# The last layer's causal mask: zeros selected by GpSimd in the exponentials, in place of mask products by TensorE in the exponent step

## The chip, the core and the metric

The kernel runs on one core of a Trainium2 chip. The metric is the device time in microseconds (us) of one execution; lower is better. Five engines of the core run in-order instruction streams side by side and meet at semaphores: TensorE (PE, matrix products into the eight PSUM banks), VectorE (DVE), ScalarE (ACT, activation functions), GpSimd (POOL, elementwise work on SBUF tiles, it does not read PSUM here) and SyncE (SP, which issues the transfers).

## The reference, cut to what matters

Four blocks are added to x in turn: a softmax attention of x over a context, an attention whose projections are a mixture of experts, a rotary cross attention, and a last layer. The last layer is the one that the change touches. It has 16 heads of 8 channels, 16 sequences of 128 tokens, a causal mask, and behind it a mixture of eight experts:

```
wei = jnp.einsum('bhtf,bhsf->bhts', q, k) * d ** (-0.5)
mask = jnp.tril(jnp.ones((t, t), bool))
wei = jnp.where(mask, wei, -jnp.inf)
wei = jax.nn.softmax(wei, axis=-1)
attn = jnp.einsum('bhts,bhsf->bhtf', wei, v)
...
y = x + layernorm(attn, ln1_g, ln1_b)
combine = top-2 of softmax gates;  h = relu(y W1 + b1);  moe = sum_e combine_e (h W2 + b2)_e
out = y + layernorm(moe, ln2_g, ln2_b)
```

## The kernel before

**Tiling.** The 16 sequences are worked in eight jobs of SPS=2 sequences. Five lanes (0 to 4) hold a job each, with buffers of their own; lanes 0 to 2 take a second job afterwards. A sixth lane (5, MOE) runs the expert products of one job after the other, and a seventh splits W1 at the start. `way(lane)` lists a lane's steps, and the string `ORDER` says, one digit per step, which lane goes next. All engines walk the same list `STEPS`, each issuing its own part of a step, so a step's place in the list is its place in every engine's stream. `TAKEN` deals out the PSUM banks in the same way.

**Attention of a layer L (B, C or D).** For each of the two sequences there is a step M: TensorE makes the scores with the query in the partitions, in four banks (q = 0 to 3, four heads each), and VectorE takes the maximum of each row (L1041). The maxima are transposed (hop "mt"). Then come two steps for each sequence. Step E (`scores` with q_first False): TensorE makes the scores again with the key in the partitions, adding the negative maximum by a product with `two` and `mT` (L622, then L630), and ScalarE writes the exponentials of bank after bank to `probs` (L816), a ring of 8 slots of 128x512 that lies in the tile `w1f`. Step PV (`weighted`, L644): TensorE multiplies `probs` by the values, 8 products for each q; it waits for `s_exp` before each q. After the second PV ScalarE copies the result (L823) and hop "pt" transposes it (L548).

**The mask.** In layer D, both M and E put a mask product first: for each of four blocks of 32 partitions and each bank q, one product of a 32x32 table (`lowS`, or `lowST` in E) by a 32x512 spread table adds -60000 to the scores that are to be masked (L613). That makes 16 products for a step; the products after it accumulate on it. There are 16 steps M and 16 steps E in layer D, one for each sequence.

**GpSimd's stream.** GpSimd turns variances into scale and shift of each norm (step ln1, L1075 to L1078; the step moe_end does the same for the last norm), ranks the gate logits (hops "B.lg" and "D.lg", L1086 to L1093), adds rows (L1113, L1129, L1132, L1134), writes `ylo` (L1136) and the output rows (L1144, L1146). It had nothing to do in a step E. ScalarE's normalisation (L781, step ln2) waits for L1078; VectorE's choice of experts (`pick`, L879 to L902) waits for L1093, and TensorE's transpose L567 waits for that.

## Time and profile before

| | |
|---|---|
| median of three runs | 498.88 us (498.03 to 503.34) |
| the profiled execution | 499.3 us, of which the profile's span 497.5 us |
| TensorE (PE) busy | 461.8 us, 93% of the span |
| ScalarE (ACT) busy | 367.8 us, 74% |
| VectorE (DVE) busy | 307.3 us, 62% |
| GpSimd (POOL) busy | 159.9 us, 32% |

The profile is one execution. A "busy" engine has an instruction in flight; the products of TensorE overlap each other, so the sum of their durations is larger than its busy time. A timeline row gives the start in us from the start of the span, the length in us, the engine, the line of the kernel, the operation, the tile written and the tiles read, their shapes, how many instructions of one kind the row merges (x16), and in square brackets how long the engine had been idle before and what released it.

### The profile page before, as it was taken

Reading aid. Unit: us, or ns where it says so; the run is one execution under the profiler, and the core shown is the slowest. Engines: PE = TensorE matmul, PEld = TensorE weight load, DVE = VectorE, ACT = ScalarE, POOL = GpSimd, SP = SyncE. Lnnn points to the kernel's source line nnn. Section 1 sums busy time; section 2 is a strip of 40 time slices with the busy share of each in tenths; the row PEclk is TensorE's granted clock in tenths of the full one; section 3 lists DMA queues with packets and bytes.
Section 4 is the critical chain, followed back from the end, with each engine's and each line's share of the span. In section 5 each row is a group of like instructions: output and inputs, shape, how many; then the busy total and the mean of one; then the engine's idle time right before and its main releaser. Section 6 shows DMA issues by size and latency. Waiting matters only on the chain.

```text
span 497.5 us, 18057 instructions
## 1 busy us (share of the span) xinstructions
PE 461.8 (93%) x7501; PEld 379.9 (76%) x7501; DVE 307.3 (62%) x941; ACT 367.8 (74%) x906; POOL 159.9 (32%) x400
## 2 busy tenths in 40 slices
PE   7768889989989999999999999999999999999793
PEld 5635476666667988897878888898798888899793
DVE  4378997978877774667875684647634736333211
ACT  5586778888888897877779878776977576675452
POOL 6662342123234422326242134141221421332302
PEclk9688999999999999999999999999999999999998
DMA  6930000000000000000000000000000000000000
GB/s 192 389 110 1 9 3 10 9 3 3 3 3 13 2 14 3 13 1 14 2 13 3 3 2 4 13 1 3 14 3 1 3 12 4 1 12 1 12 2 11
DMA packets 7928, 11.38 MB, mean 23 GB/s; under 512 B 592, under 2 KB 7208, under 8 KB 7464
## 3 DMA queue, kind: packets, MB, share of 16 engines
q1 hardware_dynamic: 7848, 10.23, 6.2%
q8 instruction: 60, 0.98, 0.9%
q14 instruction: 20, 0.16, 0.1%
HBM read 9.18 MB, written 1.05 MB: 21 GB/s over the span
## 4 chain that ended last, share of the span: by engine, by line
PE 74%; DVE 13%; POOL 6%; ACT 3%; issue 3%; DMA 0%; POOLq 0%; DVEq 0%; ACTq 0%
PE bk L654 23%; PE bk L644 6%; PE bk L699 6%; DVE negmax L1041 6%; PE bk L700 5%; PE bk L701 5%; PE bk L630 4%; PE bk L585 2%; PE bk L622 2%; PE bk L613 2%; PE bk L548 2%; PE bk L488 2%; PE bk L554 1%; PE bk L534 1%; PE bk L497 1%
## 5 line engine op out<-in xcount | busy, mean ns | idle before, releaser
L654 PE MATMUL bk<-w2f,hT 128*128 128x128 f32 x1024 | 135.6, 276 | 1.0 <-ACT hT L842 1.0
L842 ACT ACTIVATE hT<-bk,pk 128x256 f32<-128x256 f32 x256 | 107.6, 477 | 38.9 <-PE bk L701 38.4
L654 PEld LDWEIGHTS bk<-w2f,hT 128*128 128x128 f32 x1024 | 124.1, 192 | 3.9 <-ACT hT L842 1.3
L1041 DVE TENSOR_REDUCE negmax<-bk 128x4 f32<-128x512 f32 (+1 forms) x192 | 104.9, 610 | 12.7 <-PE bk L630 12.2
L816 ACT ACTIVATE w1f<-bk 128x512 f32<-128x512 f32 (+1 forms) x192 | 98.8, 600 | 18.2 <-PE bk L630 17.9
L972 DVE SCALAR_TENSOR_TENSOR acc<-bk,comb,acc 128x128 f32<-128x128 f32 x128 | 38.8, 344 | 74.9 <-PE bk L654 74.7
L699 PE MATMUL bk<-yhi,w1hi 128*128 128x256 f16 x256 | 70.1, 274 | 0.0
L701 PE MATMUL bk<-yhi,w1lo 128*128 128x256 f16 x256 | 69.8, 273 | 0.0
L700 PE MATMUL bk<-ylo,w1hi 128*128 128x256 f16 x256 | 69.8, 272 | 0.0
L1075 POOL TENSOR_SCALAR shift<-mv 128x2 f32<-128x2 f32 x40 | 9.4, 235 | 143.3 <-DVE mv L982 142.4
L644 PE MATMUL bk<-w1f,val 128*32 128x128 f32 (+1 forms) x1536 | 51.0, 275 | 0.2 <-DVE negmax L1041 0.2
L630 PE MATMUL bk<-qk 32*128 32x128 f16 (+2 forms) x1536 | 46.8, 213 | 1.6 <-DVE hl L1028 0.4
L644 PEld LDWEIGHTS bk<-w1f,val 128*32 128x32 f32 (+1 forms) x1536 | 39.4, 109 | 6.7 <-issue 2.3
L802 ACT ACTIVATE qk<-bk 128x512 f16<-128x512 f32 x72 | 37.9, 603 | 6.0 <-PE bk L585 6.0
L630 PEld LDWEIGHTS bk<-qk 32*128 32x128 f16 (+1 forms) x1536 | 32.1, 96 | 12.5 <-issue 6.5
L1086 POOL TENSOR_TENSOR qkf<-lg 128x16 f32<-128x16 f32 (+1 forms) x32 | 8.4, 284 | 76.9 <-DVE lg L867 44.8
L699 PEld LDWEIGHTS bk<-yhi,w1hi 128*128 128x128 f16 x256 | 25.6, 100 | 6.0 <-issue 1.4
L622 PE MATMUL bk<-hl,hf 32*128 32x128 f16 (+1 forms) x768 | 29.0, 218 | 0.9 <-ACT hl L766 0.5
L1077 POOL TENSOR_TENSOR rstd<-ve,neghalf 128x2 f32<-128x2 f32 x40 | 28.5, 713 | 3.3
L622 PEld LDWEIGHTS bk<-hl,hf 32*128 32x128 f16 (+1 forms) x768 | 19.9, 99 | 10.3 <-issue 7.5
L701 PEld LDWEIGHTS bk<-yhi,w1lo 128*128 128x128 f16 x256 | 25.0, 98 | 2.9
L700 PEld LDWEIGHTS bk<-ylo,w1hi 128*128 128x128 f16 x256 | 25.1, 98 | 2.8
(150 smaller groups left out, 783.7 us busy)
## 6 DMA issues: line engine op xcount, KB each, us to landing
w1f<-in_w SPq DMA_DIRECT2D x1, 2048.0 KB, 15.1
w2f<-in_w SPq DMA_DIRECT2D x1, 2048.0 KB
pk<-in_pack SPq DMA_DIRECT2D x1, 1690.0 KB, 8.1
xin<-in_x SPq DMA_DIRECT2D x8, 128.0 KB, 2.6
out<-outb SPq DMA_DIRECT2D x8, 128.0 KB, 1.8
ctxT<-in_turned SPq DMA_DIRECT2D x8, 77.0 KB, 2.4
cin<-in_ctx SPq DMA_DIRECT2D x8, 77.0 KB
hf<-in_half SPq DMA_DIRECT2D x1, 416.0 KB, 10.4
```

The costliest lines, as they stand in the source:

```text
L622: mm(score_bank(q, t == 0 and L != "D")[0:nk, t * T:(t + 1) * T], H("two")[rows_, t * T:t * T + nk], mT[s][rows_, i * T:(i + 1) * T], star ...
L630: last = mm(o, qs if q_first else ks, ks if q_first else qs, start=q_first and L != "D", stop=L != "D" or t == NT - 1)
L644: last = mm(o[32 * t:32 * t + 32, (2 * i + a) * T:(2 * i + a + 1) * T], val[s][0:nk, m, SHIFT * r:SHIFT * r + 32], probs[0:nk, ring(n, q), ...
L654: last = mm(o[:, i * D:(i + 1) * D], hT[:, k % HRING, i * T:(i + 1) * T], w2f[:, k, :], start=c == 0 and i == 0, stop=c == CH - 1, skip_gr ...
L699: mm(o[:, m * W:(m + 1) * W], hi, yhi[s][:], start=True, stop=False)
L700: mm(o[:, m * W:(m + 1) * W], hi, ylo[s][:], start=False, stop=False)
L701: last = mm(o[:, m * W:(m + 1) * W], lo, yhi[s][:], start=False, stop=True)
L802: act.activation(qk[s][:, :, t, :], bank(g, st, t)[:].rearrange("p (n w) -> p n w", n=2), ACT.Copy).then_inc(s_stk_act, 1)
L816: act.activation(probs[0:nk, ring(n, q), :], bank(g, st, q)[0:nk, :], ACT.Exp, scale=SCALE[L]).then_inc(s_exp, 1)
L842: act.activation(hT[:, k % HRING, :], bank(g, st)[:, m * W:(m + 1) * W], ACT.Relu, bias=P("b1")[:, k:k + 1]).then_inc(s_relu, 1)
L972: last = dve.scalar_tensor_tensor(out=acc[:, i, :], in0=products(j, e)[:, i * D:(i + 1) * D], scalar=comb[j % LANES][:, i, e:e + 1], in1=a ...
L1041: dve.tensor_reduce(negmax[s][:, i, NT * q:NT * (q + 1)], bank(g, st, q)[:, 0:NT * nk].rearrange("p (t k) -> p t k", t=NT), X_AXIS, ALU.ma ...
```

## The change

The exponent step of layer D no longer issues the 16 mask products: `masked` is true for M alone, and in E the product by `two` (L622, now L626) opens the accumulation in each bank instead of L613. The exponentials of layer D therefore hold values also where the mask is to act. GpSimd gets a part in step E of layer D: for q = 0 to 3 it waits for ScalarE's exponential (`s_exp`), runs one `affine_select` over the slot of `probs` in place (128x512, float32: a key later than the query becomes 0.0), and counts up the new semaphore `s_causal`. TensorE's PV in layer D waits for `s_causal` in place of `s_exp`; in layers B and C nothing changes. `TURN` counts the E steps of one layer, as `NUMBER` counts all of them. The five semaphores `s_mixT` of the lanes become one, with `TURN` as its count, which makes room for the new one; the instructions that signal and wait there stay where they were. The tables `lowST` and `spreadST` are still loaded. The string `ORDER` is the same.

```
-        pe.wait_ge(s_mixT[s], g + 1)
+        pe.wait_ge(s_mixT, TURN[g, ("top", s, "B")] + 1)
...
-                if L == "D":
-
-                    low, spread = ("lowS", "spreadS") if q_first else ("lowST", "spreadST")
+                masked = L == "D" and q_first
+                if masked:
+
+                    low, spread = "lowS", "spreadS"
                     for c in range(NT):
...
-                            mm(score_bank(q, t == 0 and L != "D")[0:nk, t * T:(t + 1) * T], H("two")[rows_, t * T:t * T + nk],
-                               mT[s][rows_, i * T:(i + 1) * T], start=L != "D", stop=False)
+                            mm(score_bank(q, t == 0)[0:nk, t * T:(t + 1) * T], H("two")[rows_, t * T:t * T + nk],
+                               mT[s][rows_, i * T:(i + 1) * T], start=True, stop=False)
...
                 for q in range(NQ):
-                    pe.wait_ge(s_exp, NQ * n + q + 1)
+                    if L == "D":
+                        pe.wait_ge(s_causal, NQ * TURN[g, ("E",) + st[1:]] + q + 1)
+                    else:
+                        pe.wait_ge(s_exp, NQ * n + q + 1)
...
+                elif kind == "E" and st[2] == "D":
+                    n = NUMBER[g, st]
+                    for q in range(NQ):
+                        pool.wait_ge(s_exp, NQ * n + q + 1)
+                        p3 = probs[:, ring(n, q), :].rearrange("p (t k) -> p t k", t=NT)
+                        pool.affine_select(p3, p3, [[0, NT], [1, T]], ALU.is_ge, 0.0, base=0, channel_multiplier=-1
+                                           ).then_inc(s_causal, 1)
```

How the streams change. First TensorE's stream at the second E step of lane 0 in layer D; L613 are the mask products, L622 those with the maxima, L630 the scores, and each row is one instruction or several alike, with the semaphores that it waits for. Before:

```order
L613 MATMUL bk<-hf 32x512 [waits s_stk_act]
L613 MATMUL bk<-hf 32x512 [waits s_read4]
L613 MATMUL bk<-hf 32x512 [waits s_stk_act]
L613 MATMUL bk<-hf 32x512 [waits s_stk_dve]
L613 MATMUL bk<-hf 32x512 x12
L622 MATMUL bk<-hl,hf 128x128 x4
L630 MATMUL bk<-qk 128x128 x4
L622 MATMUL bk<-hl,hf 128x128 x4
L630 MATMUL bk<-qk 128x128 x4
L622 MATMUL bk<-hl,hf 128x128 x4
```

After the change (L622 is now L626, L630 is L634):

```order
L626 MATMUL bk<-hl,hf 128x128 [waits s_stk_act]
L626 MATMUL bk<-hl,hf 128x128 [waits s_read4]
L626 MATMUL bk<-hl,hf 128x128 [waits s_stk_act]
L626 MATMUL bk<-hl,hf 128x128 [waits s_stk_dve]
L634 MATMUL bk<-qk 128x128 x4
L626 MATMUL bk<-hl,hf 128x128 x4
L634 MATMUL bk<-qk 128x128 x4
L626 MATMUL bk<-hl,hf 128x128 x4
```

The 16 mask products are gone, and the waits for the four free banks have moved to the first products with the maxima. Next TensorE's stream at the PV step of lane 0 (the weighted values of its first sequence, L644). Before, it waits for the exponentials alone:

```order
L585 MATMUL bk<-hl,hf 128x256 x12
L644 MATMUL bk<-w1f,val 32x128 [waits s_exp]
L644 MATMUL bk<-w1f,val 32x128 x3
L644 MATMUL bk<-w1f,val 32x128 [waits s_exp]
L644 MATMUL bk<-w1f,val 32x128 x3
```

After the change that line is L651; of the same kind of step in layer D:

```order
L588 MATMUL bk<-hl,hf 128x256 x12
L651 MATMUL bk<-w1f,val 32x128 [waits s_causal,s_exp]
L651 MATMUL bk<-w1f,val 32x128 x3
L651 MATMUL bk<-w1f,val 32x128 [waits s_causal]
L651 MATMUL bk<-w1f,val 32x128 x3
```

The two quarters left out go on in the same way. All four groups of products wait for GpSimd now; `s_exp` in the first row is the wait for a free bank. Last GpSimd's stream around the first two E steps of lane 0 in layer D; L1075 to L1078 are the scale and shift of a norm, and L1129 adds a row of constants. Before:

```order
L1076 TENSOR_SCALAR ve<-mv 128x2
L1077 TENSOR_TENSOR rstd<-ve,neghalf 128x2 [waits c_pool]
L1078 TENSOR_TENSOR shift<-shift,rstd 128x2 [waits c_pool]
L1129 TENSOR_TENSOR wc<-wc,rw 128x256 [waits s_xn1]
L1075 TENSOR_SCALAR shift<-mv 128x2 [waits s_mv4]
L1076 TENSOR_SCALAR ve<-mv 128x2
L1077 TENSOR_TENSOR rstd<-ve,neghalf 128x2 [waits c_pool]
L1078 TENSOR_TENSOR shift<-shift,rstd 128x2 [waits c_pool]
L1075 TENSOR_SCALAR shift<-mv 128x2 [waits s_mv3]
```

After the change (L1075 is now L1082, L1129 is L1143):

```order
L1084 TENSOR_TENSOR rstd<-ve,neghalf 128x2 [waits c_pool]
L1085 TENSOR_TENSOR shift<-shift,rstd 128x2 [waits c_pool]
L1139 AFFINE_SELECT w1f<-w1f 128x512 [waits s_exp] x4
L1143 TENSOR_TENSOR wc<-wc,rw 128x256 [waits s_xn1]
L1139 AFFINE_SELECT w1f<-w1f 128x512 [waits s_exp] x4
L1082 TENSOR_SCALAR shift<-mv 128x2 [waits s_mv4]
L1083 TENSOR_SCALAR ve<-mv 128x2
L1084 TENSOR_TENSOR rstd<-ve,neghalf 128x2 [waits c_pool]
L1085 TENSOR_TENSOR shift<-shift,rstd 128x2 [waits c_pool]
```

The selections stand at the place of the E step, four for each, and the norms of lanes 4 and 3 (`s_mv4`, `s_mv3`) stand behind the second four.

## Rows read from the trace of the kernel before

**Rows 1.** The profile's slices: TensorE's busy tenths in 40 slices of the span.

```profile
PE   7768889989989999999999999999999999999793
```

**Rows 2.** Windows: busy us of each engine, then granted clock, DMA share, GB/s.

```profile
125.00:440.00 315.00, 309.24 (x5296) 261.90 (x5295) 196.81 (x601) 245.38 (x598) 98.90 (x241) 1.00 0.02 6
440.00:497.00 57.00, 46.95 (x420) 44.19 (x418) 13.74 (x53) 27.74 (x68) 11.85 (x26) 0.97 0.02 6
```

**Rows 3.** TensorE's waits from 125 to 440 us, longest: total, times, longest.

```profile
PE bk L567 <- DVE comb L902: 1.4, 2, 0.7
```

**Rows 4.** Timeline: the first E step of layer D and its PV.

```profile
125.71 0.43 PE L613 MATMUL bk<-hf 32*32 32x512 f16 x16
126.08 0.23 PE L622 MATMUL bk<-hl,hf 32*128 32x128 f16 x4
126.75 2.06 ACT L816 ACTIVATE w1f<-bk 128x512 f32<-128x512 f32 x4 [0.34 <-PE bk L630]
129.39 0.32 PE L644 MATMUL bk<-w1f,val 128*32 128x128 f32 x4
```

**Rows 5.** GpSimd's groups by shape: count, busy us, mean ns, idle before.

```profile
L1129 POOL TENSOR_TENSOR wc<-wc,rw 128x256 f32<-128x256 f32 x8 | 5.8, 728 | 1.0 <-ACT wc L781 1.0
L1108 POOL MEMSET val<- 128x1024 f32 x5 | 4.8, 952 | 0.0
L1076 POOL TENSOR_SCALAR ve<-mv 128x2 f32<-128x2 f32 x40 | 8.9, 222 | 2.5
L1089 POOL TENSOR_SCALAR qkf<-qkf 128x128 f32<-128x128 f32 x8 | 4.3, 538 | 0.7
L1124 POOL CAST hl<-qkf 128x154 f16<-128x154 f32 x8 | 3.0, 380 | 0.5
```

**Rows 6.** Timeline: the second pair, the norm on GpSimd beside it, what follows.

```profile
131.40 0.23 POOL L1075 TENSOR_SCALAR shift<-mv 128x2 f32<-128x2 f32 x1 [7.79 <-DVE mv L982]
...
131.92 2.06 ACT L816 ACTIVATE w1f<-bk 128x512 f32<-128x512 f32 x4
...
133.75 1.08 PE L644 MATMUL bk<-w1f,val 128*32 128x128 f32 x32
...
134.11 0.90 ACT L781 ACTIVATE xn<-xin,shift,rstd 128x128 f32<-128x128 f32 x2
...
134.90 0.60 ACT L823 ACTIVATE qk<-bk 128x512 f32<-128x512 f32 x1
...
135.65 0.63 PE L548 MATMUL bk<-pk,qk 128*128 128x128 f32 x4 [0.24 <-ACT qk L823]
```

**Rows 7.** Timeline: the third pair, gate ranks on GpSimd, the transpose behind them.

```profile
144.96 2.07 ACT L816 ACTIVATE w1f<-bk 128x512 f32<-128x512 f32 x4
...
145.62 0.54 POOL L1086 TENSOR_TENSOR qkf<-lg 128x64 f32<-128x64 f32 x2 [6.01 <-DVE lg L867]
...
147.62 1.08 PE L644 MATMUL bk<-w1f,val 128*32 128x128 f32 x32
...
148.23 0.46 POOL L1093 TENSOR_TENSOR qkf<-qkf 128x128 f32<-128x128 f32 x1
...
150.35 0.38 PE L567 MATMUL bk<-pk,comb 128*8 128x128 f32 x2 [0.73 <-DVE comb L902]
```

**Rows 8.** Timeline: the eleventh pair, with the last norm's scale on GpSimd.

```profile
353.35 2.07 ACT L816 ACTIVATE w1f<-bk 128x512 f32<-128x512 f32 x4 [0.43 <-PE bk L630]
...
355.31 0.20 POOL L1078 TENSOR_TENSOR shiftF<-shiftF,rstdF 128x2 f32<-128x2 f32 x1
...
355.71 1.08 PE L644 MATMUL bk<-w1f,val 128*32 128x128 f32 x32
```

**Rows 9.** Timeline: the sixteenth and last pair, the same norm beside it.

```profile
432.21 2.06 ACT L816 ACTIVATE w1f<-bk 128x512 f32<-128x512 f32 x4 [1.88 <-PE bk L630]
...
434.16 0.20 POOL L1078 TENSOR_TENSOR shiftF<-shiftF,rstdF 128x2 f32<-128x2 f32 x1
...
434.43 1.08 PE L644 MATMUL bk<-w1f,val 128*32 128x128 f32 x32
```

More of the change, by code:

```diff
@@ L155, in schedule @@
     ways, at = [way(lane) for lane in range(PRE + 1)], [0] * (PRE + 1)
-    steps, counts, number, taken, last = [], {}, {}, {}, {}
+    steps, counts, number, turns, taken, last = [], {}, {}, {}, {}, {}
     banks = iter(TAKEN)
@@ L165, in schedule @@
         counts[step[0]] = number[g, step] + 1
+        turns[g, step] = counts.get((step[0], step[2:3]), 0)
+        counts[step[0], step[2:3]] = turns[g, step] + 1
         for slot in range(uses(step)):
@@ L171, in schedule @@
     assert all(at[lane] == len(ways[lane]) * rounds(lane) for lane in range(PRE + 1))
-    return steps, number, taken
-STEPS, NUMBER, BANK = schedule()
+    return steps, number, turns, taken
+STEPS, NUMBER, TURN, BANK = schedule()
 assert all(NUMBER[g, ("E",) + st[1:]] == NUMBER[g, st] for g, st in STEPS if st[0] == "PV")
@@ L310, in build @@
         s_rank = per_lane(sem, "s_rank")
-        s_mixT = per_lane(sem, "s_mixT")
+        s_mixT = sem("s_mixT")
         s_mixed = per_lane(sem, "s_mixed")
@@ L332, in build @@
         s_outb, s_store = sem("s_outb"), sem("s_store")
+        s_causal = sem("s_causal")
         s_passed = sem("s_passed")
@@ L627, in scores @@
                         ks = qk[s][rows_, 1, t, i * T:i * T + nk]
-                        b = score_bank(q, q_first and t == 0 and L != "D")
+                        b = score_bank(q, q_first and t == 0 and not masked)
                         o = b[:, t * nk:(t + 1) * nk] if q_first else b[0:nk, t * T:(t + 1) * T]
-                        last = mm(o, qs if q_first else ks, ks if q_first else qs, start=q_first and L != "D",
-                                  stop=L != "D" or t == NT - 1)
+                        last = mm(o, qs if q_first else ks, ks if q_first else qs, start=q_first and not masked,
+                                  stop=not masked or t == NT - 1)
                 last.then_inc(s_mfull if q_first else s_efull, 1)
@@ L894, in mixers @@
                                              ALU.mult, ALU.mult)
-                last.then_inc(s_mixT[s], 1)
+                last.then_inc(s_mixT, 1)
             def weigh(g, s, E, dst):
```

## The prediction

> **What bounds the kernel now.** I read the slices first, to see who is full where, then the windows, then TensorE's own waits, and last the timeline at the sixteen places that the change touches. TensorE is at nine tenths or more in nearly every slice [rows 1]. From 125 to 440 us, where all E steps of layer D lie, it is busy for 309.2 of 315 us, ScalarE for 245.4, VectorE for 196.8 and GpSimd for 98.9 [rows 2]. Its longest wait there, summed, is 1.4 us in two places, for the experts' weights [rows 3]. So TensorE sets the pace there with under 6 us of gaps: what is taken from its stream shortens the run, and any time at which it stands still in its queue lengthens it, since nothing overtakes a waiting product. The last 57 us hold no attention. The granted clock is 1.00 from 125 to 440 us [rows 2], the 2.4 GHz level, and I expect no change of it from stalls of 1 to 4 us.
>
> **What is removed.** The 16 mask products of one E step lie four by four in different parts of the array and largely run together: from their start at 125.71 to the next product at 126.08 is 0.37 us [rows 4]. The same distance stands at fifteen of the sixteen E steps (0.53 at one), together 6.1 us. All of it lies on TensorE's path, so this is a gain of **6.1 us**, and the most that the change can give. The sixteen M steps keep theirs. The one semaphore in place of five for `s_mixT` moves nothing: I cost it at zero, since VectorE signals in the order in which TensorE waits.
>
> **What one selection costs.** No row shows it, so I bound it. Below: the fill of 128x1024 takes 0.95 us, and it reads nothing; half as many columns cannot be had for less than 0.48 us. Above: the one-input comparison takes 0.222 us for 2 columns and 0.538 us for 128, which is 2.5 ns a column and gives 1.50 us for 512; the two-input addition of 256 columns, 0.73 us, doubled is 1.46. Between them, the cast (0.380 us for 154 columns against the same 0.222) has 1.04 ns a column and gives 0.75 us. All are in [rows 5]. A selection compares and chooses at each element, so it should be dearer than the cast; but it need not be written as badly as the comparison. I take c = **0.95 us**, near the middle of 0.48 and 1.50, and keep both ends.
>
> The Trainium skill, GPSIMD Engine Reference, section 4.1 (Engine selection) calls one-input work on GpSimd roughly line-rate, and its section 7 (Performance pitfalls for Q7 kernels) gives a compare-and-select body 1.03 cycles an element when it is unrolled. By these 512 columns would take about 0.44 us and a dispatch, an estimate from that page; the sum would then be that of the second case below. The trace agrees for the cast (1.04 ns a column) and not for the comparison (2.5 ns).
>
> **What TensorE waits for now.** ScalarE's four exponentials start 0.49 us apart and the first is out 0.60 us after the start (four end at 2.06). One GpSimd instruction for each of them at 0.95 us is slower than the exponentials come, so the last selection ends 0.60 + 4c, and about 0.1 for two handovers (my estimate), after the exponentials' start. PV takes 1.08 us in four quarters [rows 6], so its last quarter starts 0.8 us after its first. PV that now starts a gap G after the exponentials' start is therefore held up by 4c - 0.1 - G, if that is positive. The gap is 129.39 - 126.75 = 2.64 at the first E step [rows 4] and 434.43 - 432.21 = 2.22 at the last [rows 9]; in order the sixteen are 2.6, 1.8, 2.7, 3.4, 6.3, 2.0, 8.2, 2.9, 10.9, 4.0, 2.4, 6.1, 2.5, 2.2, 3.6, 2.2. With c = 0.95 what is needed is 3.7, and twelve fall short, by 0.1 to 1.9: together **12.5 us**. Only the four long gaps, where expert products lie between E and PV, cover the selections. Before, the same gaps covered the exponentials (2.06 against a last quarter at G + 0.8).
>
> **GpSimd is late at three places.** A selection must also wait for what stands ahead of it in GpSimd's queue. At the eleventh pair the last norm's scale ends at 355.51, and the first exponential had been out since 353.95 [rows 8]; at the sixteenth it is 434.36 against 432.81 [rows 9]; at the thirteenth it is the same distance. Each time the four selections begin 1.5 us later: **4.5 us** more. The norm's input comes from TensorE's own products, so these stay in step.
>
> **What waits behind the selections.** (a) Second pair: the scale of lane 4's norm, now at 131.40 [rows 6], stands behind selections that end at 131.92 + 0.65 + 3.8 = 136.4, and takes 1.6 us (four instructions) to 138.0. ScalarE stands at its normalisation for it (now 134.11), and behind that stands the copy of PV's result (now 134.90), which then ends at about 139.5. TensorE's transpose of it, now at 135.65, is due at 137.5 with the stall of 1.9 counted above, so 2.1 us more. (b) Third pair: the gate ranks, now 145.62 to 148.69, begin at 149.4 and end at 152.5; VectorE's five small steps up to the transpose took 1.7 us, so L567 starts at 154.2 and not at 150.35, or 151.0 with the stall counted and a further mask gone [rows 7]. That is 3.2 us more, and the pair after it loses its 0.3. (c) Others of this kind are shorter or have expert products over them; I put 1 us for them, and take 1.5 off because later waits shrink when everyone else gets ahead. Together **about 4.5 us**. The row additions (L1129 and the like) move by up to 8 us too, but are read many steps later, so I cost them at nothing; if `base` were late, the load of a lane's next job would be.
>
> **Sum.** -6.1 + 12.5 + 4.5 + 4.5 = +15.4 us. The profiled execution took 499.3 us, 0.4 above the median of 498.9; on the median that is 514.3, and I say **515 us**.
>
> **The rivals.** Case 1, the forecast: c between 0.7 and 1.3. By the same sums the stalls of the pairs and the late starts are 8 to 35 us, less 6.1, and with the queue's share 503 to 533 us. For it speak the rows of GpSimd's comparison and addition. Chance 0.63.
> Case 2, a cheap selection, c from 0.48 to 0.7: at 0.6 the gaps fall short by 1.0 in all, the three late places bring this to 5.3, the queue costs perhaps 1; less 6.1 that is nothing. 498 to 503 us. For it speaks the cast, against it the comparison. Chance 0.20.
> Case 3, faster: GpSimd keeps pace with the exponentials (c below 0.5), the selection ends half a us after the last exponential, and at the three late places the norm moves forward with TensorE's gain. Then the 6.1 us stay, 493 us. The rows of short gaps (1.8 and 2.0 us) speak against even that, and the fill, which reads nothing, would be slower than this. The point from which it decides is c = 0.49, the pace of the exponentials. Chance 0.05.
> Case 4, a dear selection, c from 1.3 to 1.5 or above: at 1.5 the gaps fall short by 38.6 us, 43 with the late starts, the queue's share grows to about 10; 499 - 6 + 53 = 546 us. The comparison row speaks for it. Chance 0.12.
>
> **The numbers.** The likeliest case gives 515 us. The range of 500 to 533 holds case 1 and most of case 2, and leaves out case 3, case 4 and the low end of case 2, about 2 in 10. A measurement of this kernel tells about 1%, 5 us, from no change. Faster by over 1% is case 3, 0.05. Within 1% (494 to 504) is case 2 and a corner of case 1, 0.20. Slower is the rest, 0.75.
>
> **What the profile after would show.** No L613 in E steps (half of its 512 products). A GpSimd group of 64 selections, whose mean is c: this decides most. In TensorE's waits a new first row, PV (now L651) for the selection, of 12 to 20 us in a dozen or so places, longest near 4 us. Larger waits of ScalarE for L1078's successor and of the transpose L567's successor for the experts' weights. GpSimd busy for about 220 us. I would be wrong if c is below 0.7, if GpSimd starts a new operation with a pause, or if the stalls are given back elsewhere, which TensorE's gaps allow for 6 us at most [rows 2].

## The result and the profile after

The changed kernel is **slower: ratio 1.0274 to the kernel before, 95% interval 1.0180 to 1.0368**. That it is slower is clear; whether by more than 2% the interval leaves open. Its median is 514.38 us (511.69 to 517.9, four executions), against 501.05 us for the kernel before, measured with it (498.03 to 503.34, four executions). The profiled execution took 514.0 us, of which the span is 512.3 us, and is 14.7 us above the profiled one of before. The number on record, 515 us, is within 1 us. The way to it is not the one on record, as will be seen.

The page of the changed kernel begins like this (busy us, share of the span, number of instructions; below the granted clock of TensorE in 40 slices of the span, where 9 stands for nine tenths or more of 2.4 GHz, and in the second fence the same row of the kernel before):

```profile
span 512.3 us, 17610 instructions
...
PE 469.5 (92%) x7245; PEld 383.5 (75%) x7245; DVE 309.0 (60%) x941; ACT 367.6 (72%) x906; POOL 198.4 (39%) x464
...
PEclk9667999999977999999999999999999999999898
```

```profile
PEclk9688999999999999999999999999999999999998
```

TensorE has 256 instructions fewer and GpSimd 64 more. TensorE's clock, new against [rows 2], falls in the twelfth and thirteenth slice, from 141 to 167 us, and a little in the 38th. Next the two groups that are new or changed (count, busy us, mean ns of one, then idle time before it and who ended it):

```profile
L651 PE MATMUL bk<-w1f,val 128*32 128x128 f32 (+1 forms) x1536 | 56.1, 282 | 5.1 <-POOL w1f L1139 4.7
...
L1139 POOL TENSOR_SCALAR_AFFINE_SELECT w1f<-w1f 128x512 f32<-128x512 f32 x64 | 39.1, 646 | 32.9 <-ACT w1f L823 32.9
```

A selection takes 0.646 us on average, and a block of four 2.40 us, so one every 0.60 us: much less than the 0.95 us of the forecast. The selections do not slow the other engines' own work by anything that the averages show: the exponentials take 601 ns (600 before), VectorE's maxima 611 (610 before). So what is lost is waiting, and the clock. TensorE's waits from 120 to 460 us (total us, times, longest) show three large ones in place of the 1.4 us of [rows 3]:

```profile
PE bk L651 <- POOL w1f L1139: 4.7, 17, 0.8
PE bk L570 <- DVE comb L909: 4.0, 2, 3.3
PE bk L551 <- ACT qk L830: 2.6, 3, 2.2
```

**Where the time went.** The same products stand in the same order in both traces, apart from the mask products that are gone. So each product of TensorE can be matched with its partner, and the difference of their starts, each from the start of its span, is the lag of the changed kernel. It grows where time is lost. The columns below are places by the time of the kernel before: the lag there is that of the first matched product at or behind that time, and the last column is the last product. The rows anticipate the experiments, which are described further on, and are computed in the same way. Each row is one execution, the profiled one.

| kernel, lag in us at | 120 | 140 | 165 | 240 | 345 | 410 | 440 | end |
|---|---|---|---|---|---|---|---|---|
| changed kernel | 0.8 | 3.5 | 9.1 | 9.6 | 9.7 | 13.3 | 14.4 | 14.8 |
| no selection (e1) | 0.1 | 0.0 | 1.3 | 0.6 | -0.6 | -1.1 | -1.4 | 1.2 |
| selections and products (e2) | 2.3 | 6.2 | 12.4 | 13.4 | 14.2 | 18.2 | 21.0 | 21.8 |
| no selection, gaps filled (e9) | -0.5 | -0.6 | -0.7 | -1.5 | -2.7 | -3.1 | -3.5 | -3.5 |
| before, gaps filled (e11) | 0.3 | 0.3 | 0.2 | 0.1 | 0.1 | 0.1 | 0.1 | 0.1 |
| queue only (e3) | -0.2 | 3.0 | 8.0 | 7.4 | 7.5 | 7.1 | 6.7 | 6.7 |
| half width (e4) | 0.8 | 2.6 | 8.3 | 7.8 | 6.9 | 7.8 | 8.1 | 8.1 |
| first four (e5) | 0.1 | 2.8 | 8.3 | 8.3 | 8.3 | 8.3 | 8.2 | 8.2 |
| last twelve (e6) | -1.1 | -1.1 | -1.1 | -0.5 | -0.4 | 3.9 | 5.1 | 5.5 |
| gaps filled (e7) | 0.2 | 2.7 | 4.8 | 5.4 | 5.5 | 9.1 | 10.3 | 10.3 |
| norm after (e12) | -0.5 | 2.6 | 7.6 | 8.2 | 11.9 | 16.2 | 19.7 | 19.7 |

The first column stands ahead of every exponent step of layer D. It is how an execution's start went, within about 1 us, and 2.3 us in e2. Of the 14.8 us of the changed kernel, 8.3 come between 120 and 165 us, at four of the sixteen pairs of exponent step and PV, and 5.3 between 165 and 440 us.

**The second pair.** This is the changed kernel's timeline, for comparison with [rows 6]:

```profile
132.39 0.25 DVE L989 BATCH_NORM_AGGREGATE mv<-stats 128x2 f32<-128x6 f32 x2
...
132.67 2.06 ACT L823 ACTIVATE w1f<-bk 128x512 f32<-128x512 f32 x4
...
133.34 2.40 POOL L1139 TENSOR_SCALAR_AFFINE_SELECT w1f<-w1f 128x512 f32<-128x512 f32 x4 [2.39 <-ACT w1f L823]
...
135.79 0.43 PE L651 MATMUL bk<-w1f,val 128*32 128x128 f32 x8 [0.16 <-POOL w1f L1139]
135.82 0.24 POOL L1082 TENSOR_SCALAR shift<-mv 128x2 f32<-128x2 f32 x1
...
137.44 0.88 ACT L788 ACTIVATE xn<-xin,shift,rstd 128x128 f32<-128x128 f32 x2 [2.43 <-POOL shift L1085]
...
138.23 0.57 ACT L830 ACTIVATE qk<-bk 128x512 f32<-128x512 f32 x1
...
138.94 0.63 PE L551 MATMUL bk<-pk,qk 128*128 128x128 f32 x4 [2.15 <-ACT qk L830]
...
140.58 1.94 PE L651 MATMUL bk<-w1f,val 77*32 77x128 f32 x32
```

PV itself waited little: the lag grows by 0.6 us across it. But the norm that stood at 131.40 before, whose input was there at 132.6 (first row), is taken up by GpSimd at 135.82, behind the selections. ScalarE stands for it for 2.43 us, with the copy of PV's result queued behind it, and TensorE stands for that copy for 2.15 us. The last row shows what nobody had counted: the next block of 32 products takes 1.94 us, where the same 32 products took 1.08 before, because the granted clock has fallen to 0.50, the 1.2 GHz level.

**The third and fourth pair**, against [rows 7]:

```profile
150.06 2.40 POOL L1139 TENSOR_SCALAR_AFFINE_SELECT w1f<-w1f 128x512 f32<-128x512 f32 x4 [7.17 <-ACT w1f L823]
...
152.44 0.54 POOL L1093 TENSOR_TENSOR qkf<-lg 128x64 f32<-128x64 f32 x2
...
155.11 0.45 POOL L1100 TENSOR_TENSOR qkf<-qkf 128x128 f32<-128x128 f32 x1
...
156.65 0.17 DVE L909 TENSOR_TENSOR comb<-picked,lmax 128x16 f32<-128x16 f32 x1
156.98 0.58 PE L570 MATMUL bk<-pk,comb 128*8 128x128 f32 x2 [3.31 <-DVE comb L909]
...
161.26 1.94 PE L651 MATMUL bk<-w1f,val 128*32 128x128 f32 x32
```

The gate ranks begin 2.5 us after their input (the logits were there at 149.95), right behind the selections, and TensorE stands for 3.31 us in place of 0.73. Again the clock falls. These windows of the changed kernel (from:to, length, busy us and count of TensorE, its weight loads, VectorE, ScalarE and GpSimd, then the granted clock) show both falls:

```profile
136.00:140.00 4.00, 1.85 (x60) 1.05 (x52) 1.47 (x3) 2.56 (x6) 2.54 (x8) 0.96 0.00 0
140.00:144.00 4.00, 4.00 (x97) 2.88 (x82) 3.86 (x11) 2.56 (x7) 1.35 (x4) 0.50 0.01 4
144.00:148.00 4.00, 4.00 (x62) 3.08 (x58) 2.05 (x6) 2.66 (x7) 0.00 (x0) 0.69 0.00 0
...
156.00:160.00 4.00, 3.02 (x13) 2.40 (x14) 2.62 (x11) 0.38 (x1) 3.92 (x7) 0.59 0.02 4
160.00:164.00 4.00, 4.00 (x74) 2.71 (x73) 2.33 (x6) 1.57 (x4) 1.46 (x5) 0.56 0.12 35
```

TensorE was busy for 1.85 of 4 us, then its clock was at half. The Trainium skill, TensorE: Matmul & The Clock Gate, Part 1 (The HAM clock gate), puts it so: "the default state is throttled, and activity releases the throttle". The trace agrees in the direction: 1.00 in the stretches before the gaps, 0.50 in the stretches behind them.

**The eleventh pair**, against [rows 8]:

```profile
362.68 2.06 ACT L823 ACTIVATE w1f<-bk 128x512 f32<-128x512 f32 x4
...
365.00 0.20 POOL L1085 TENSOR_TENSOR shiftF<-shiftF,rstdF 128x2 f32<-128x2 f32 x1
365.14 2.41 POOL L1139 TENSOR_SCALAR_AFFINE_SELECT w1f<-w1f 128x512 f32<-128x512 f32 x4
...
365.94 0.93 PE L651 MATMUL bk<-w1f,val 128*32 128x128 f32 x16 [0.82 <-POOL w1f L1139]
...
367.61 0.42 PE L651 MATMUL bk<-w1f,val 128*32 128x128 f32 x8 [0.17 <-POOL w1f L1139]
```

Here PV does wait for the selections, because they begin late: the exponentials started at 362.68, so the first was out at 363.3, and GpSimd is at the last norm until 365.2. The lag goes from 9.3 us ahead of this PV to 11.2 at its end. The same is seen at the 13th and the 16th, behind the same norm, and at the 14th, where additions to the output rows (L1158 and L1160) stand ahead of the selections.

### The profile page after: what moved, and what is told of

Same layout as the page of the kernel before. It is cut to its first block, busy times and chain, and to the rows that moved or that the text cites. A ratio compares the mean times of both kernels' runs of the same rounds, so it can differ in the third digit from the quotient of the medians.

```text
span 512.3 us, 17610 instructions
## 1 busy us (share of the span) xinstructions
PE 469.5 (92%) x7245; PEld 383.5 (75%) x7245; DVE 309.0 (60%) x941; ACT 367.6 (72%) x906; POOL 198.4 (39%) x464
## 4 chain that ended last, share of the span: by engine, by line
PE 69%; POOL 12%; DVE 11%; ACT 4%; issue 3%; POOLq 0%; DVEq 0%
PE bk L661 22%; PE bk L706 6%; PE bk L708 5%; PE bk L707 5%; PE bk L651 5%; DVE negmax L1048 4%; POOL w1f L1139 4%; PE bk L634 3%; PE bk L588 2%; PE bk L626 2%; PE bk L551 2%; PE bk L476 2%; PE bk L491 2%; PE bk L500 1%; POOL rstd L1084 1%
## 5 line engine op out<-in xcount | busy, mean ns | idle before, releaser
L1048 DVE TENSOR_REDUCE negmax<-bk 128x4 f32<-128x512 f32 (+1 forms) x192 | 105.1, 611 | 13.2 <-PE bk L634 12.5
L651 PE MATMUL bk<-w1f,val 128*32 128x128 f32 (+1 forms) x1536 | 56.1, 282 | 5.1 <-POOL w1f L1139 4.7
L1082 POOL TENSOR_SCALAR shift<-mv 128x2 f32<-128x2 f32 x40 | 9.4, 234 | 120.3 <-DVE mv L989 119.0
L651 PEld LDWEIGHTS bk<-w1f,val 128*32 128x32 f32 (+1 forms) x1536 | 39.6, 112 | 16.7 <-POOL w1f L1139 8.4
L1139 POOL TENSOR_SCALAR_AFFINE_SELECT w1f<-w1f 128x512 f32<-128x512 f32 x64 | 39.1, 646 | 32.9 <-ACT w1f L823 32.9
L634 PE MATMUL bk<-qk 32*128 32x128 f16 (+2 forms) x1536 | 48.4, 217 | 1.7 <-DVE hl L1035 0.6
L634 PEld LDWEIGHTS bk<-qk 32*128 32x128 f16 (+1 forms) x1536 | 33.1, 98 | 13.4 <-issue 7.3
L626 PE MATMUL bk<-hl,hf 32*128 32x128 f16 (+1 forms) x768 | 29.3, 220 | 0.9 <-ACT hl L773 0.5
L788 ACT ACTIVATE xn<-xin,shift,rstd 128x128 f32<-128x128 f32 x48 | 21.0, 495 | 12.0 <-POOL shift L1085 12.0
## 6 DMA issues: line engine op xcount, KB each, us to landing
w1f<-in_w SPq DMA_DIRECT2D x1, 2048.0 KB, 14.7
```

The costliest lines, as they stand in the source:

```text
L626: mm(score_bank(q, t == 0)[0:nk, t * T:(t + 1) * T], H("two")[rows_, t * T:t * T + nk], mT[s][rows_, i * T:(i + 1) * T], start=True, stop= ...
L634: last = mm(o, qs if q_first else ks, ks if q_first else qs, start=q_first and not masked, stop=not masked or t == NT - 1)
L651: last = mm(o[32 * t:32 * t + 32, (2 * i + a) * T:(2 * i + a + 1) * T], val[s][0:nk, m, SHIFT * r:SHIFT * r + 32], probs[0:nk, ring(n, q), ...
L1048: dve.tensor_reduce(negmax[s][:, i, NT * q:NT * (q + 1)], bank(g, st, q)[:, 0:NT * nk].rearrange("p (t k) -> p t k", t=NT), X_AXIS, ALU.ma ...
L1139: pool.affine_select(p3, p3, [[0, NT], [1, T]], ALU.is_ge, 0.0, base=0, channel_multiplier=-1).then_inc(s_causal, 1)
```

## The experiments

In what follows a pair is one exponent step of layer D with its PV, numbered 1 to 16 in order of time. Each ratio is to the kernel before as measured together with that run; medians that were not measured together are less well comparable. Which pairs have selections is set by these lines, here as in e5 (the other runs have another condition in the last two; all sixteen stand in SELECTED unless a run says otherwise):

```
PAIRS = [x for x in STEPS if x[1][0] == "E" and x[1][2] == "D"]
SELECTED = [x for n, x in enumerate(PAIRS, 1) if n <= 4]
PRODUCTS = [x for n, x in enumerate(PAIRS, 1) if n > 4]
```

My theory (A) was that TensorE sets the pace, so that the mask products are worth their 6 us, and that the loss has three parts: PV waiting where GpSimd starts late, other work late behind the selections in GpSimd's queue, and the clock behind the stalls. The rivals were that the products' gain is not real (C), and that the loss is PV's own waits, wherever the gap is short (B).

### e1: no selection, no mask products

SELECTED is empty, and PV waits for the exponentials alone.

```
-                    if L == "D":
-                        pe.wait_ge(s_causal, ...)
-                    else:
-                        pe.wait_ge(s_exp, NQ * n + q + 1)
+                    pe.wait_ge(s_exp, NQ * n + q + 1)
...
-                elif kind == "E" and st[2] == "D":
+                elif kind == "E" and (g, st) in SELECTED:
```

> The changed kernel with the selections left out: no mask at all in the exponent step of layer D, PV waits for the exponentials as before (so the last layer's attention is not masked). It measures the gain term alone. Theory A (TensorE sets the pace, so the 16 x 0.37 us of mask products are a gain): 6 us below the kernel before, ratio 0.988. Rival C (the mask products lay under other waits, the gain is not real): no difference, ratio 1.000 to 0.996.

Measured: ratio 1.000 (0.9969 to 1.0031), median 500.65 against 500.17 us. **My theory missed here, and the rival C had it right in number.** The lag shows why, in two parts. First, in the first four pairs the products' time is taken by other waits: the lag is -0.39 behind an exponent step and back at -0.02 at the next transpose. After 165 us it falls from 1.34 to -1.45, that is 2.8 us of the twelve times 0.37 = 4.4 us. Second, the clock fell twice where it had not before, and this took the rest back: 1.4 us at 153 us, and 2.7 us at 465 us, in a place that no mask product is near. These are the windows of e1 and then of the kernel before:

```profile
140.00:165.00 25.00, 22.10 (x380) 17.52 (x379) 18.14 (x58) 20.88 (x52) 9.19 (x22) 0.93 0.03 8
...
440.00:480.00 40.00, 37.49 (x311) 34.79 (x310) 9.98 (x37) 20.35 (x51) 8.44 (x18) 0.91 0.02 4
```

```profile
140.00:165.00 25.00, 22.84 (x424) 18.27 (x423) 19.09 (x61) 22.36 (x55) 9.21 (x22) 1.00 0.03 8
...
440.00:480.00 40.00, 37.38 (x336) 35.15 (x335) 10.57 (x41) 21.83 (x54) 9.04 (x20) 1.00 0.02 4
```

### e2: selections and mask products

Both lists hold all sixteen pairs.

```
-                masked = L == "D" and q_first
+                masked = L == "D" and (q_first or (g, st) in PRODUCTS)
...
-                               mT[s][rows_, i * T:(i + 1) * T], start=True, stop=False)
+                               mT[s][rows_, i * T:(i + 1) * T], start=not masked, stop=False)
```

> The changed kernel with the mask products put back into the exponent step beside the selections. It measures the cost of the selections alone. Theory A: the changed kernel plus the 6 us of the products, some 19 to 20 us above the kernel before, ratio 1.040. Rival C: the same time as the changed kernel, ratio 1.027.

Measured: ratio 1.035 (1.0274 to 1.0426), median 518.2 us. It lies between the two expectations: the products add 3.8 us to the changed kernel by the medians (518.2 against 514.4), not 6 and not 0. That leans to the half of them which e1's lag shows to be on the path, but the intervals of the two kernels overlap. The traces do not settle it either: by the lag from 120 to 440 us e2 loses 5.1 us more than the changed kernel, but its profiled execution is the slowest of five (521.1 us), and its clock is down for longer (a mean of 0.73 from 138 to 170 us, against 0.79, and 0.91 from 450 to 490, against 0.96).

### e3: GpSimd's queue without PV's wait

The selections read a constant tile and write a tile that nobody reads; they wait for the exponentials as before, and PV waits for the exponentials alone, as in e1.

```
+        aside = sb("aside", [128, 2, NT, T])
...
                     for q in range(NQ):
+                        after(pool, s_causal, NQ * TURN[g, st] + q - 1)
                         pool.wait_ge(s_exp, NQ * n + q + 1)
-                        p3 = probs[:, ring(n, q), :].rearrange("p (t k) -> p t k", t=NT)
-                        pool.affine_select(p3, p3, ...)
+                        src3 = P("w0")[:, 0:NT * T].rearrange("p (t k) -> p t k", t=NT)
+                        pool.affine_select(aside[:, q % 2], src3, ...)
```

> The changed kernel, but the 64 selections wait for the exponentials, read a constant tile and write a tile that nobody reads, and PV waits for the exponentials alone (the last layer's attention is not masked). GpSimd's queue is as full as in the changed kernel, and only PV's wait is gone. Theory A (two mechanisms: PV's own waits where GpSimd is late, and norms and gate ranks that stand behind the selections in GpSimd's queue from 130 to 160 us, with a fall of TensorE's clock behind each stall): the second part stays, about +7.5 us up to 165 us, and the rest of the run gains its mask products, -3.5 us: +4 us, ratio 1.008. Rival B (the loss is PV's waits alone): as fast as without selections, -6 us, ratio 0.988.

Measured: ratio 1.0116 (1.0054 to 1.0179), median 506.32 us. Rival B falls: with no wait of PV for GpSimd at all the kernel is still about 6 us slower than before. TensorE's waits from 120 to 460 us are

```profile
PE bk L574 <- DVE comb L910: 4.0, 2, 3.4
PE bk L555 <- ACT qk L831: 3.3, 3, 2.9
```

the same two as in the changed kernel. By the lag 8.2 us come between 120 and 165 us, as in the changed kernel (8.3), although there PV had waited too: what PV does not wait at the second pair, the transpose behind it waits (2.9 in place of 2.2 us). From 165 to 440 us the lag of e3 falls by 1.3 us where that of the changed kernel grows by 5.3, so PV's own waits are 6.6 us, all of it after 165 us. Theory A's 1.008 lies in the interval, but its 3.5 us of gain after 165 us came out as 1.3.

### e4: selections of half the width

```
-                        pool.affine_select(p3, p3, [[0, NT], [1, T]], ...)
+                        pool.affine_select(p3[:, 0:2, :], p3[:, 0:2, :], [[0, 2], [1, T]], ...)
```

> The changed kernel with each selection over two of the four heads of its slot, half the columns (the other two heads stay unmasked). Expected duration of one by the two-point line of this engine's rows: about 0.35 us, less than the 0.49 us between two exponentials. Theory A: the direct waits go, the waits at the late places shrink to 0.7 us each and the queue's part shrinks only by the 0.6 us by which a block of four ends earlier: +8 us against the kernel before, ratio 1.016. Rival B (the width of a selection decides everything): close to the kernel without selections, -4 us or lower, ratio 0.990.

Measured: ratio 1.0133 (1.0065 to 1.0201), median 507.4 us. The selections' own row, seen by line (shortest, median and longest ns):

```profile
L1142 POOL TENSOR_SCALAR_AFFINE_SELECT w1f<-w1f x64: 406/409/739, 127.9 to 442.9; 128x256 f32<-128x256 f32 x64
```

0.409 us for 256 columns against a median of 0.635 for 512 is 0.88 ns a column and 0.18 us beside. The Trainium skill, GPSIMD Engine Reference, section 7 (Performance pitfalls for Q7 kernels), gives 1.03 cycles an element for an unrolled compare-and-select body, which is an estimate of 0.86 ns a column by the working of the prediction (0.44 us for 512). The trace's 0.88 ns agrees with it; whether the selection runs such a body no run here shows. Theory A (1.016) lies in the interval, rival B (0.990) does not. With half the width 7.5 us are still lost between 120 and 165 us, against 8.3, and nothing net after it, against 5.3; TensorE's waits for the selections are down from 4.7 to 1.2 us. The selections' length thus has little effect in the first part, and decides the second.

### e5 and e6: the first four pairs, the last twelve

> Selections in the first four exponent steps of layer D only (125 to 160 us); the other twelve use mask products as before. Theory A (the norms and gate ranks behind the selections, and TensorE's clock behind the stalls, lose about 8 us between 130 and 165 us, in these four alone): 8 us above the kernel before, ratio 1.016. Rival B (each step costs about the same where its gap is short, that is 12 places): 3 to 5 us, ratio 1.008.

> The opposite half: mask products in the first four exponent steps of layer D, selections in the other twelve. Theory A: the waits at the late places (1.4 us each at pairs 11, 13, 14 and 16, less twelve times 0.37) remain, 5 to 6 us above the kernel before, ratio 1.011, and TensorE's clock stays at 1.00 between 140 and 165 us. Rival B: 9 us or more, ratio 1.018.

Measured: e5 1.0152 (1.0083 to 1.0220), median 507.68 us; e6 1.0118 (1.0039 to 1.0196), 505.75 us. Both are as theory A has them, and together (1.5 and 1.2%) they make up the whole 2.7%. The windows from 140 to 165 us, of e5 and then of e6:

```profile
140.00:165.00 25.00, 21.02 (x345) 15.78 (x346) 15.98 (x48) 15.42 (x38) 12.42 (x26) 0.75 0.03 8
```

```profile
140.00:165.00 25.00, 23.68 (x433) 19.21 (x433) 18.05 (x58) 22.34 (x56) 9.22 (x22) 1.00 0.03 8
```

The clock falls exactly where the first four have selections. In e5 the lag does not move after 165 us: what is lost early is not given back.

### e7: the changed kernel with its gaps filled

```
+EXTRA = {(0, 0, "D.pt"): 14, (0, 0, "D.cT"): 24}
...
+                if (g, s, h) in EXTRA:
+                    fill(o, EXTRA[g, s, h])
                 after(pe, s_read[s], read(g, h) - 1)
...
+                    o = take_bank(pe, g, st)
+                    if g == JOBS - 1:
+                        fill(o, 12)
                     pe.wait_ge(s_read[s], read(g // LANES, "D.cT"))
-                    o = take_bank(pe, g, st)
```

> The changed kernel with products by a constant tile in three gaps of TensorE, ahead of its waits: 14 before the transpose of lane 0's first result (gap of 2.15 us), 24 before the transpose of its experts' weights (gap of 3.31 us), 12 before the last job's first product (gap of 1.58 us). They give nothing to the result and end inside the gaps. Theory A (part of the loss is the fall of the granted clock from 2.4 to 1.2 GHz behind these gaps, 1.1 + 2.6 us by the lag of TensorE's products): the clock stays at 1.00 from 140 to 165 us and the kernel is 3 to 4 us faster than the changed one, ratio 1.019 to the kernel before. Rival D (the stalls alone are the loss, the clock only shows them): same time as the changed kernel, 1.027, or slower for the products that were added.

Measured: ratio 1.0207 (1.0133 to 1.0282), median 509.94 us, 4.4 us below the changed kernel by the medians and 3.4 by the ratios; the intervals overlap, and it is the trace that decides. The same window, with 0.73 in the changed kernel (first fence) and 1.00 in e7 (second):

```profile
140.00:165.00 25.00, 21.02 (x359) 15.81 (x344) 15.94 (x46) 15.78 (x39) 12.42 (x26) 0.73 0.03 8
```

```profile
140.00:165.00 25.00, 22.13 (x420) 17.25 (x412) 18.91 (x60) 18.74 (x46) 13.84 (x30) 1.00 0.03 8
```

From 120 to 165 us e7 loses 4.6 us and the changed kernel 8.3. So the two falls of the clock are worth 3.7 us, and the stalls themselves 4.6. Rival D falls.

### e8: selections only where the gap is long

Pairs 5, 7, 9, 10, 12 and 15 have selections, the others mask products.

> Selections only at the six exponent steps with a gap of at least 3.6 us to their PV (the 5th, 7th, 9th, 10th, 12th and 15th), mask products at the other ten. Theory A: PV never waits, six times 0.37 us are gained, and about 0.5 us is lost behind the fifth; 1.5 us below the kernel before, ratio 0.997, unless a gap costs a fall of the clock. Rival C (what the products leave behind is taken by other waits or by the clock): no difference, ratio 1.000.

Measured: ratio 0.9993 (0.9955 to 1.0031), median 500.85 us. No difference that the times can tell. In the trace PV never waits and the lag falls by 1.6 us from 120 to 440 us, as expected; then the clock falls behind the last job's start (0.91 from 440 to 480 us) and the lag returns from -2.8 to -0.2. That is again a place where the kernels do not differ.

### e9, e10, e11: the gaps filled without the selections' stalls

e9 is e1, e10 is e8, and e11 is the kernel before in all that computes; each has fills before the transpose of lane 0's first experts' weights (8, 6, 6) and before the last job's first product (12).

> No mask in the exponent step of layer D (neither products nor selections, so the last layer's attention is not masked), and products by a constant tile in two gaps: 8 before the transpose of lane 0's first experts' weights, 12 before the last job's first product. It asks where the 6.1 us of the mask products went. Theory A (3 us of them are real on TensorE's path after 165 us, the rest was taken by other waits, and falls of the clock behind the gaps at 150 and 460 us took the 3 us back): with the clock held, 2.5 to 3 us below the kernel before, ratio 0.994. Rival E (nothing of the products is on the path): ratio 1.000.

> The version that the runs point to: selections only at the six exponent steps with a long gap, mask products at the other ten, and the products by a constant tile in the two gaps (6 and 12). Theory A: 1.5 us from the selections and, where an execution of the kernel before has a fall of the clock in its last part, up to 2.6 us more; ratio 0.995. Rival E: ratio 1.000.

> The kernel before in all that computes (mask products at all sixteen exponent steps, no selection), with the products by a constant tile in the same two gaps (6 and 12). The control for the run with covered selections. Theory A: as fast as the kernel before where that has no fall of the clock, else up to 2.6 us faster: ratio 0.998, and the covered selections 1.5 us below it.

Measured: e9 0.9946 (0.9925 to 0.9966), median 496.21 us; e10 0.9986 (0.9965 to 1.0008), 498.32 us; e11 1.0006 (0.9992 to 1.0020), 499.42 us; before 499.32 us. The window of e9 in the last part, against 0.91 in e1:

```profile
440.00:480.00 40.00, 38.69 (x348) 36.33 (x347) 9.78 (x37) 21.04 (x53) 7.67 (x16) 1.00 0.02 5
```

e9 answers what the mask products are worth: **2.9 us, not 6.1** (lag from -0.51 to -3.45; 0.2 of it in the first four pairs, 2.7 in the other twelve, where short waits, most of them at the 11th to the 16th, take the rest of the gain back). e11 also shows that the one semaphore in place of five for `s_mixT`, which all these runs have, costs nothing that can be seen. Of e1's missing gain about half was never there, and the other half went to the clock. e10 is 1.1 us below e11 by the medians, as the six covered pairs should give, but its interval holds 1.000. So no version with the mask in place is shown to be faster than the kernel before; e9, which leaves it out of the exponent step, is.

### e12: the last norm behind the selections

Where the scale of the last norm stands directly ahead of selections in GpSimd's order (pairs 7, 11, 13 and 16), the two change places.

```
+                if st[0] == "moe_end":
+                    a = order.index((g, st))
+                    b = next((n for n in range(a + 1, len(order)) if pool_works(order[n])), None)
+                    if b is not None and order[b][1][0] == "E":
+                        order.insert(b, order.pop(a))
```

> The changed kernel with one exchange in GpSimd's order: where the scale and shift of the last norm stand directly ahead of a block of selections (the 7th, 11th, 13th and 16th pair), they come after it. Theory A (selections that start 1.9 us late at three short gaps cost 1.4 us each): these waits go, PV waits by under 0.3 us there, up to 4 us faster than the changed kernel, ratio 1.019. Rival F (ScalarE's normalisation, which then waits 2.5 us longer for the scale, holds the experts' activations and TensorE behind them): given back, ratio 1.025 to 1.028, with new waits of TensorE for the activations.

Measured: ratio 1.0437 (1.0401 to 1.0472), median 520.53 us. Both expectations missed: the exchange costs 6 us more by the medians (8 by the ratios, 5 by the profiled executions), and rival F is right in kind but too small. TensorE's waits from 120 to 460 us, of which the first, fourth and fifth are new, while PV's falls from 4.7 to 0.9:

```profile
PE bk L664 <- ACT hT L852: 5.1, 3, 2.4
PE bk L573 <- DVE comb L912: 4.0, 2, 3.3
PE bk L554 <- ACT qk L833: 2.6, 3, 2.2
PE bk L629 <- ACT acc L845: 2.4, 1, 2.4
PE bk L709 <- ACT acc L845: 2.2, 1, 2.2
PE bk L654 <- POOL w1f L1155: 0.9, 3, 0.6
```

At the eleventh pair:

```profile
365.52 2.41 POOL L1155 TENSOR_SCALAR_AFFINE_SELECT w1f<-w1f 128x512 f32<-128x512 f32 x4 [15.53 <-ACT w1f L826]
...
369.41 0.20 POOL L1088 TENSOR_TENSOR shiftF<-shiftF,rstdF 128x2 f32<-128x2 f32 x1
369.64 0.88 ACT L791 ACTIVATE zF<-acc,shiftF,rstdF 128x128 f32<-128x128 f32 x2 [2.72 <-POOL shiftF L1088]
370.55 0.38 ACT L845 ACTIVATE acc<-bk 128x256 f32<-128x256 f32 x1
...
370.99 0.23 PE L629 MATMUL bk<-hl,hf 32*128 32x128 f16 x2 [2.42 <-ACT acc L845]
```

The selections start on time, and the norm ends at 369.6. ScalarE stands for it, the copy that empties a bank stands behind it, and TensorE stands for 2.42 us for that bank, where PV's own waits had been 1.1. It confirms that the late start is the cause of PV's wait at these pairs (the wait is gone). Of the two orders tried, each makes TensorE stand: GpSimd's block of 2.4 us found no free place at either.

## Why the prediction was right, and where it was not

The time and its direction were right, and the agreement to 1 us is luck: three terms of the sum were off by much, and they cancelled. The time fell into the range of case 1 (503 to 533 us), but the condition of that case, a selection of 0.7 to 1.3 us, was not met; the cost was that of case 2, whose sum gave 498 to 503. The prediction's own sign of being wrong, c below 0.7, came true. With the measured cost the prediction's own sum gives about nothing (case 2), and four terms then make up the difference: the products are worth 3.2 us less, the queue costs 6.2 and not 1, the waits of PV 6.6 and not 5.3, and the clock 3.7. The mechanisms that it named (PV waiting for selections, late starts behind the norm, norms and ranks late behind the selections) were all found, and the fall of the clock was missed. The ledger, in us, by the profiled executions:

| step | forecast | measured | from |
|---|---|---|---|
| mask products gone | -6.1 | -2.9 | e9 |
| PV waits at short gaps, and at late places | 12.5 + 4.5 | 6.6 | changed kernel less e3, after 165 us |
| behind the selections in the queue, early | 4.5 | 4.8 | e7 (4.6) and the 0.2 of e9, 120 to 165 us |
| the same, after 165 us | in the 4.5 | 1.4 | e3 (-1.3) less e9 (-2.7) |
| TensorE's clock | 0 | 3.7 | changed kernel less e7, 120 to 165 us |
| start and end of the execution | 0 | 1.2 | the lag at 120 us (0.8) and after 440 us (0.4) |
| sum | 15.4 | 14.8 | |

The rows are differences between single executions, taken in one order, and executions of one kernel differ by some us; a tenth of a us in them says nothing. That the products are worth 2.9 us is shown without the selections; beside them (e2) it may be more.

- **"This is a gain of 6.1 us, all of it on TensorE's path"** failed. It is 2.9. In the first four pairs TensorE had other waits close behind (busy 22.8 of 25 us from 140 to 165 before), and they took all but 0.2 of 1.5 us. Of the other 4.4 us 2.7 were real. I had read the busy share of the whole stretch [rows 2], and it hides the 2.2 us of gaps in these 25 us.
- **"I take c = 0.95 us"** failed: one selection took 0.646 us, 0.60 in a block. I had given 0.20 to a cost below 0.7, and by that case's sum the time would have been 498 to 503 us. The cast's row (0.75 us by its line) was the nearest, and even that was above it; the fill's (0.48) was below. The 2.5 ns a column came from two different operations, an addition of 2 columns and a comparison of 128; the comparison alone, at 32 and 128 columns of the same line (314 and 538 ns), gives 2.3. Either way it said nothing about the selection.
- **"Twelve fall short, together 12.5 us"** failed with it. (By the gaps as listed it is eleven.) With 0.60 the formula gives 1 us, and the trace shows 0.6 at the second pair, 1.2 at the sixth (where one selection took 1.08 us) and none at the eighth.
- **"GpSimd is late at three places, 4.5 us"** was right in kind: there are four (11, 13, 14 and 16), late by 1.3 to 1.9 us, and the lag grows by 1.5 to 1.9 us across each of these PV steps, which is as much as the 6.6 us net. e12 shows the cause for the norm (11, 13 and 16); no run moved the additions at the 14th by themselves.
- **"(a) 2.1 us more" and "(b) 3.2 us more"** held in place and nearly in size: the lag steps by 1.9 us at the second pair's transpose and by 2.6 at the experts' weights. They held although c was wrong: in the prediction's own steps a shorter block moves PV and the work behind it together.
- **"I expect no change of the clock from stalls of 1 to 4 us"** failed: it fell behind the 2.15 and the 3.31 us, and cost 3.7 us.
- **"A new first row in TensorE's waits, 12 to 20 us"** failed as a sign: it is the first row, but of 4.7 us. That alone should make a reader distrust the 12.5. GpSimd was busy for 198 us, not 220, for the same reason.

What stays open: which of two like gaps is followed by a fall of the clock. The gap of 1.58 us ahead of the last job, with one of about 1 us behind it, is the same in the kernel before and in e1; the profiled execution of e1 has a fall behind it worth 2.7 us, that of before none. And the 0.9 us that the changed kernel and e3 lose at about 275 us, behind a wait for an activation (0.2 in e4), I have not followed up; in e3 they are most of the 1.4 us of the fourth row.

## What to carry to other kernels

Work that is moved to an idle engine is paid for in that engine's queue: ask what stands ahead of it when its input comes and what stands behind it while it runs, and follow the late piece to the engine that sets the pace. Here GpSimd was busy for 32% of the span, yet 39 us of selections cost some 16.5 us, the clock's share included, against a gain of 3. Cut a stretch at its gaps before calling an engine its bound: products taken out beside a gap only widened the gap, and gaps that grow can bring the clock down.

## What the runs showed of the hardware

- A selection of zeros by GpSimd (affine_select, float32, in place) took 0.635 us for 128x512 and 0.409 us for 128x256 (medians), 0.88 ns a column; the comparison of [rows 5] took 2.3 ns a column on the same engine (314 ns for 32 columns, 538 for 128).
- TensorE's granted clock fell from 2.4 to 1.2 GHz behind gaps of 2.15 and 3.31 us in a run in which TensorE was busy for 92% of the span, and for 1.85 of the 4 us around the first of them; 32 products then took 1.94 us in place of 1.08. Fourteen and 24 products by a constant tile in these gaps kept it at 1.00, and were worth 3.7 us.
- The same gap (1.58 us, ahead of the last job) was followed by a fall in the profiled executions of e1 and e8 and by none in that of the kernel before; the falls cost 2.7 and 2.6 us. For this kernel that is about as much as the whole gain of the mask products.
